# A mixture of experts on one core: experts of a chunk accumulated in one PSUM bank, with the router weight behind the GELU

## What is computed

```python
def _L0_ffn_ref(x, gate_w, gate_b, W1, b1, W2, b2):
    logits = xf @ gate_w + gate_b
    probs = jax.nn.softmax(logits, axis=-1)
    top2_vals, top2_idx = jax.lax.top_k(probs, 2)
    cw = jnp.zeros((N, Ee), dtype=xf.dtype).at[jnp.arange(N)[:, None], top2_idx].add(top2_vals)

    def step(acc, params):
        w1, bb1, w2, bb2, we = params
        h = jax.nn.gelu(xf @ w1 + bb1, approximate=False)
        y = h @ w2 + bb2
        return (acc + we[:, None] * y, None)
    out, _ = jax.lax.scan(step, jnp.zeros_like(xf), (W1, b1, W2, b2, cw.T))
...
h = h + _L0_ffn_ref(_layernorm(h, axis=-1), ...)
```

## Time and profile before

| | us |
|---|---|
| median of 3 runs | 418.08 |
| lowest of them | 417.31 |
| span of the profiled execution | 417.87 |

### The profile page before, as it was taken

The page is one execution under the profiler, slowest core; times in us unless marked ns, Lnnn a source line. Parts: engine busy times, 40 slices in busy tenths (PEclk is TensorE's granted clock), DMA queues, the critical chain, the costliest instruction groups (busy, mean ns, idle before and its releaser), DMA issues.

```text
span 417.9 us, 11928 instructions
## 1 busy us (share of the span) xinstructions
PE 359.1 (86%) x4976; PEld 247.0 (59%) x4976; DVE 226.4 (54%) x446; ACT 198.2 (47%) x382; POOL 112.6 (27%) x138
## 2 busy tenths in 40 slices
PE   4999839999997799999587947878776997999997
PEld 1447726677775534343244527878776993477774
DVE  3277797787646743333693999946663038500002
ACT  1574235444447356776747792570008645531110
POOL 9009991000000036465133026880000003000000
PEclk9999969999998699999959995999999898899999
DMA  7400012222212122121000000000000000000001
GB/s 280 192 0 2 5 38 57 60 59 59 65 54 61 55 62 59 58 64 57 20 0 0 2 0 2 3 4 5 5 5 3 3 5 0 2 0 2 0 2 71
DMA packets 20558, 14.82 MB, mean 35 GB/s; under 512 B 2329, under 2 KB 19353, under 8 KB 20377
## 3 DMA queue, kind: packets, MB, share of 16 engines
q1 hardware_dynamic: 20504, 14.07, 10.7%
HBM read 13.32 MB, written 0.74 MB: 34 GB/s over the span
## 4 chain that ended last, share of the span: by engine, by line
PE 54%; DVE 18%; POOL 11%; issue 8%; ACT 7%; DMA 1%; SPq 0%; POOLq 0%; DVEq 0%
PE PS L763 49%; POOL arena L298 7%; PE PS L827 4%; DVE arena L710 3%; DVE arena L566 2%; DVE arena L549 2%; POOL arena L321 2%; DMA arena<-xT 1%; ACT arena L356 1%; ACT arena L353 1%; POOL arena L317 1%; ACT arena L468 1%; POOL arena L316 1%; DVE arena L713 1%; ACT arena L472 1%
## 5 line engine op out<-in xcount | busy, mean ns | idle before, releaser
L763 PE MATMUL PS<-arena,K 128*128 128x360 f32 (+2 forms) x608 | 163.1, 513 | 21.5 <-DVE arena L566 6.4
L763 PE MATMUL PS<-arena 128*45 128x45 f32 (+6 forms) x3264 | 129.9, 227 | 21.3 <-ACT arena L448 9.7
L763 PEld LDWEIGHTS PS<-arena 128*45 128x45 f32 (+3 forms) x3264 | 111.7, 133 | 40.1 <-issue 23.9
L763 PEld LDWEIGHTS PS<-arena,K 128*128 128x128 f32 (+2 forms) x608 | 75.8, 183 | 82.5 <-issue 22.1
L298 POOL TENSOR_TENSOR arena<-arena 128x360 f32<-128x360 f32 x32 | 30.0, 948 | 105.9 <-DVE arena L672 105.2
L672 DVE TENSOR_TENSOR arena<-PS,arena 128x360 f32<-128x360 f32 x32 | 17.1, 533 | 33.7 <-ACT arena L402 33.7
L763 PE MATMUL PS<-K,arena 128*45 128x32 f32 (+4 forms) x768 | 26.1, 223 | 5.1 <-DVE arena L655 4.4
L763 PEld LDWEIGHTS PS<-K,arena 128*45 128x45 f32 (+2 forms) x768 | 25.3, 132 | 7.0 <-DVE arena L655 5.0
L827 PE MATMUL PS<-K,arena 128*128 128x128 f32 x128 | 21.5, 292 | 7.8 <-ACT arena L377 7.7
L756 DVE SCALAR_TENSOR_TENSOR arena<-PS,K,arena 128x360 f32<-128x360 f32 x4 | 2.4, 593 | 47.2 <-PE PS L763 47.2
L380 ACT COPY arena<-PS 128x360 f32<-128x360 f32 x32 | 14.9, 468 | 25.5 <-PE PS L827 25.4
(11 more groups left out here) (124 smaller groups left out, 422.8 us busy)
## 6 DMA issues: line engine op xcount, KB each, us to landing
WG<-wr SPq DMA_DIRECT2D x64, 64.0 KB, 1.9
arena<-wr SPq DMA_DIRECT2D x64, 64.0 KB, 1.9
arena<-xT SPq DMA_DIRECT2D x4, 368.0 KB, 6.4
K<-consts SPq DMA_DIRECT2D x1, 1171.0 KB, 12.3
K<-consts SPq DMA_DIRECT2D x1, 852.0 KB, 9.9
out<-arena SPq DMA_DIRECT2D x4, 180.0 KB, 1.9
K<-consts SPq DMA_DIRECT2D x1, 510.0 KB, 5.5
K<-consts SPq DMA_DIRECT2D x1, 352.0 KB, 12.4
```

Of the source, the lines that this page charges most:

```text
L763: return nc.tensor.matmul(o, l, r, start=start, stop=stop)
```

## The change

Chunks become the outer loop of the mixture and experts the inner; the unit (e, c) is software-pipelined with MOE_LAG = 2: in step n PE issues hid(n), y(n-2), cwb(n). Per unit:
- hid goes to one of two pairs of banks (0, 1 or 2, 3), the GELU's result to one of three pairs of slots.
- cwb becomes two bf16 matmuls with 32 rows each, one for each half, that spread the expert's weight over all 128 partitions, into banks 4 and 5. DVE multiplies the 720 hidden values by it in place. ACT's copy is gone.
- y is a pair of matmuls that accumulate on top of b2 in one bank per chunk (6 or 7), over all eight experts. DVE adds that bank to the residual once per chunk (`acc`). POOL has no part left.
- `hid` stands behind `cw2` for all experts, and `cwT` uses banks 4 to 7.

```diff
-    stage(("hid", 0), ("cwT", 0), ("cw2", 0), ("b2", 0), ("y", 0))
-    for i in range(1, E):
-        stage(("hid", i), ("y", i))
+    stage(("cwT", 0), ("cw2", 0))
+
+    moe = [(e, c) for c in range(C) for e in range(E)]
+    for n in range(len(moe) + MOE_LAG):
+        if n < len(moe):
+            order.append(("hid", *moe[n]))
+        if n >= MOE_LAG:
+            e, c = moe[n - MOE_LAG]
+            if e == 0:
+                order.append(("b2", 0, c))
+            order.append(("y", e, c))
+            if e == E - 1:
+                order.append(("acc", 0, c))
+        if n < len(moe):
+            order.append(("cwb", *moe[n]))
...
+        def hidden(i, c):
+
+            return a(c, (slot(3), slot(6), slot(8))[unit(i, c) % 3], 2 * W)
+
+        def hid_banks(i, c):
+
+            lo = 2 * (unit(i, c) % 2)
+            return PS[:, lo:lo + 2, 0:W]
+
+        def out_bank(c):
+
+            return 6 + c % 2
...
-                elif name == "y":
-                    pool.wait_ge(sem["y_mul"], n)
-                    if i:
-                        pool.wait_ge(sem["acc"], COUNT["y", i - 1, c])
-                    g.tensor_tensor(a(c, H_), a(c, H_), a(c, slot(3 + i % 2)), ALU.add).then_inc(sem["acc"], 1)
...
-                elif name == "y":
-                    act.wait_ge(sem["y_mm"], n)
-                    s.copy(a(c, slot(8)), bank(c, 1)).then_inc(sem["cwb"], 1)
...
+                elif name == "cwb":
+                    dve.wait_ge(sem["gelu"], n)
+                    dve.wait_ge(sem["cwb_mm"], n)
+                    v.tensor_tensor(halves(hidden(i, c)), halves(hidden(i, c)), PS[:, 4:6, 0:W], ALU.mult).then_inc(
+                        sem["scaled"], 1)
+                elif name == "acc":
+                    dve.wait_ge(sem["y_mm"], COUNT["y", E - 1, c])
+                    v.tensor_tensor(a(c, H_), a(c, H_), PS[:, out_bank(c), 0:W], ALU.add).then_inc(sem["acc"], 1)
...
                 elif name == "b2":
-                    pe.wait_ge(sem["c_r"], n)
-                    mm(bank(c, 0), k("b2"), a(c, slot(5))).then_inc(sem["b2_mm"], 1)
+                    if c < 2:
+                        pe.wait_ge(sem["c_r"], COUNT["cwT", 0, 2 + c])
+                    else:
+                        pe.wait_ge(sem["acc"], c - 1)
+                    mm(PS[:, out_bank(c), 0:W], k("b2"), a(c, slot(5)), stop=False)
                 elif name == "hid":
-                    if i == 0:
+                    if n == 1:
                         pe.wait_ge(sem["g_steps"], 1)
+                    if n > 2:
+                        pe.wait_ge(sem["gelu"], n - 2)
+                    for j in range(2):
+                        last = mm(hid_banks(i, c)[:, j], k("w1", i * HID, i * HID + HID, 64 * j, 64 * j + 64),
+                                  half(c, N_, j, 0, W, 64))
+                    last.then_inc(sem["hid_mm"], 1)
+                elif name == "cwb":
+                    pe.wait_ge(sem["cwT"], COUNT["cw2", 0, c])
+                    if n == 1:
+                        pe.wait_ge(sem["c_r"], C)
                     else:
-                        pe.wait_ge(sem["y_mul"], COUNT["y", i - 1, c])
-                    for j in range(2):
-                        last = mm(bank(c, j), k("w1", i * HID, i * HID + HID, 64 * j, 64 * j + 64), half(c, N_, j, 0, W, 64))
-                    last.then_inc(sem["hid_mm"], 1)
+                        pe.wait_ge(sem["scaled"], n - 1)
+                    for j in range(2):
+                        last = mm(PS[:, 4 + j, 0:W], selb[64 * j:64 * j + 32, i * 128:i * 128 + 128],
+                                  part_bf(c, 12)[64 * j:64 * j + 32])
+                    last.then_inc(sem["cwb_mm"], 1)
                 elif name == "y":
-                    if i == 0:
-                        pe.wait_ge(sem["cwT"], n)
-                        pe.wait_ge(sem["b2_add"], n)
-                    pe.wait_ge(sem["gelu"], n)
-                    for j in range(2):
-                        mm(bank(c, 0, W, 0, 64 * j, 64 * j + 64), k("w2", i * D, i * D + D), a(c, slot(6 + j)))
-                    mm(bank(c, 1), selb[:, i * 128:i * 128 + 128], part_bf(c, 12)).then_inc(sem["y_mm"], 1)
+                    pe.wait_ge(sem["scaled"], n)
+                    for j in range(2):
+                        last = mm(PS[64 * j:64 * j + 64, out_bank(c), 0:W], k("w2", i * D, i * D + D),
+                                  hidden(i, c)[:, j * W:(j + 1) * W], start=False, stop=(i == E - 1))
+                    last.then_inc(sem["y_mm"], 1)
...
-                sel[64 * j + E * part + e, e, 64 * j:64 * j + 64] = 1
+                sel[64 * j + E * part + e, e, :] = 1
```

More of the change, by code:

```diff
@@ L68 @@
 attT_mm attT wo_mm h1
-gate_mm g_sub g_exp cw cwT_mm c_hi c_r c_mid cwT b2_mm b2_add
-hid_mm gelu y_mm cwb y_mul acc
+gate_mm g_sub g_exp cw cwT_mm c_hi c_r c_mid cwT
+hid_mm gelu cwb_mm scaled y_mm acc
 delta xi xa xi_late rk_mm rk vw_mm vw aw_mm aw_aa aw_sg ab_mm ab g_hid g_sig gg_mm gg cs ep em kk0 kk_sq kk_mm kk_cl kk_ln kk_rs
@@ L78 @@
 LAG = 2
+MOE_LAG = 2
 def schedule():
@@ L215, in gate, with unit @@
             return a(0, slot(14) + C * PP * E * r, n)
+        def unit(i, c):
+            return E * c + i
+        def hidden(i, c):
[5 more added lines that the diff above has]
+            return 6 + c % 2
         def part_bf(c, i):
@@ L390, in _ @@
                     act.wait_ge(sem["cwT_mm"], n)
-                    s.copy(part_bf(c, 10), bank(c, 1)).then_inc(sem["c_hi"], 1)
+                    s.copy(part_bf(c, 10), PS[:, 4 + c, 0:W]).then_inc(sem["c_hi"], 1)
                 elif name == "cw2":
@@ L397, in _ @@
                     act.wait_ge(sem["hid_mm"], n)
-                    s.activation(halves(a(c, slot(6), 2 * W)), both(c), ACT.Gelu,
-                                 bias=k("b1", i, i + 1)).then_inc(sem["gelu"], 1)
-                elif name == "y":
-                    act.wait_ge(sem["y_mm"], n)
-                    s.copy(a(c, slot(8)), bank(c, 1)).then_inc(sem["cwb"], 1)
+                    s.activation(halves(hidden(i, c)), hid_banks(i, c), ACT.Gelu, bias=k("b1", i, i + 1)).then_inc(
+                        sem["gelu"], 1)
                 elif name == "mixes":
@@ L658, in _ @@
                     dve.wait_ge(sem["c_hi"], n)
-                    v.scalar_tensor_tensor(out=a(c, slot(5)), in0=part_bf(c, 10), scalar=vec("cw_mid"), in1=bank(c, 1),
+                    v.scalar_tensor_tensor(out=a(c, slot(5)), in0=part_bf(c, 10), scalar=vec("cw_mid"), in1=PS[:, 4 + c, 0:W],
                                            op0=ALU.mult, op1=ALU.add).then_inc(sem["c_r"], 1)
@@ L784, in _ @@
                     ready = {"lt": ("tok_y", c + 1), "l1": ("h0", c + 1), "l2": ("h1", c + 1),
-                             "l3": ("acc", COUNT["y", E - 1, c]), "gn": ("o_ev", c + 1), "l4": ("h3", c + 1)}[LNS[i]]
+                             "l3": ("acc", c + 1), "gn": ("o_ev", c + 1), "l4": ("h3", c + 1)}[LNS[i]]
                     pe.wait_ge(sem[ready[0]], ready[1])
@@ L854, in _ @@
                     pe.wait_ge(sem["cw"], n)
-                    pe.wait_ge(sem["gelu"], COUNT["hid", 0, c])
                     for p, j in pairs:
-                        last = mm(to_bank(c, 1, T, j, p, 3 * E), a(c, CW_ + 3 * p * E, 3 * E), k("identf", 64 * j, 64 * j + T))
+                        last = mm(PS[64 * j:64 * j + 3 * E, 4 + c, T * p:T * p + T], a(c, CW_ + 3 * p * E, 3 * E),
+                                  k("identf", 64 * j, 64 * j + T))
                     last.then_inc(sem["cwT_mm"], 1)
```

## The result

| | median us | ratio to before, 95% interval |
|---|---|---|
| before | 418.95 | |
| changed, first measurement | 432.37 | 1.031 (1.027 to 1.035) |
| changed, again, beside the experiments | 433.37 (before: 420.15) | 1.031 (1.027 to 1.036) |

The change makes the kernel 3.1% slower, 13 us. The forecast was 429.0 with a range of 425.0 to 434.2.

What follows compares the result with a forecast made beforehand. PE was taken to bound the mixture. To the 417.87 us span it added 10.1 (4.8 shapes, 2.6 hid round once hidden, 2.8 head's rest, fill and tail), 0.2 for the median and 0.8 for the clock: 429.0 us, range 425.0 to 434.2.

Steps and rivals of the forecast that it cites:

- The bound: Mixture before the change: PE sets the pace, busy 6.68 of 6.68 us; removing ACT and POOL work pays only at edges.
- The stream, 1.82 us a unit: Mixture's steady state on PE: hid 0.80, y 0.76, cwb 0.26, together 1.82 us a unit, 0.15 more than before.
- one hid pair alone: A pair of hid matmuls on PE with no hid before it: 0.80 us, from 2.62 - 1.82.
- 32-to-64 step free: Rival: PE's step from 32-row cwb to 64-row hid costs no shape change; -3.2 us, 425.8 us, chance 0.10.
- The spreading pair side by side: The two 32-row cwb matmuls on PE run together, at the price of the one they replace.
- The rival in sequence: The two cwb matmuls run one after the other, adding a 0.16 us pass per unit; +5.0 us, 434.0 us, chance 0.12.
- The waits: Semaphore waits in the stream, such as cwb(n) for scaled(n-1), do not bind; scaling is 0.905 us on DVE.
- The loop around it: Spreading, DVE scaling, semaphores: 1.4 us, under 1.82; the rival that it binds gave 431.3 us, chance 0.07.
- The head: Mixture's start: first hid and GELU table load come behind the cw2 casts; PE rests 2.5 us before cwb(1).
- The clock: PE's clock may halve after the head's rest, costing 1.7 us; even odds, so 0.8 us was added.
- Span and median: Whole run: the median was taken to lie 0.2 us above the profiled execution's span, so 428.0 became 428.2.
- the three b2 in the stream: Three further b2 matmuls on PE between the mixture's units, counted at 0.80 us each.

Runs made afterwards that it cites:

- e6: Kernel before with y of two chunks ahead of their two spreading matmuls, five shape changes a round instead of nine; 416.76 us, ratio 0.992.
- e7: Kernel before with each spreading matmul cut into two of 64 columns, in the shape of y; 414.41 us, ratio 0.986.
- e1: Changed kernel with spreading matmuls of 64 rows instead of 32, one shape change fewer per unit; 429.09 us, 1.015 times before.
- e3: Changed kernel with 64-row spreading, first two hid pairs under top2, units taken in pairs, five pairs of hidden slots; 420.17 us, 0.999 times before.
- e8: Kernel before with its first round of hid moved behind cw2, stream untouched; 425.38 us, ratio 1.014.
- e2: Changed kernel with the first two hid pairs ahead of cwT again, under top2; 432.89 us, 1.029 times before.

## Why the prediction came out as it did

- **The bound.** PE, not the POOL of the chain. Shown: e6 and e7 take nothing but changes of shape out of PE's stream, and the run follows.
- **The stream, 1.82 us a unit.** Measured 1.82, part by part. Adding up starts from rows made the sum right although I read one thing too small. I priced a change at 0.10, the step ahead of the next record; the other 0.10, in hid's first weights, was inside the 0.80 of "one hid pair alone", where I did not see it. e1 put the whole at 0.20 for hid, so the rival "32-to-64 step free" would have been worth 6 us and not 3.2. It did not occur: the step was charged. The Trainium skill's rule that a change of tiling mode drains the engine (TensorEngine Tiling (Array Packing), Key Properties) fits every step of both kernels: each change was charged, and e1 and e7 show the price. That the time is a drain the traces do not show.
- **The spreading pair side by side.** Its two records start together and take 0.33. The rival in sequence is out.
- **The waits.** None binds; the scaling took 0.904 us for the 0.905 of the earlier trace rows. The loop around it is 1.49 us (e3) and not 1.4, still under 1.82.
- **The head.** The rest was forecast at 2.5 and is 2.50. The table load took 1.28, with GELU 0.02 behind it, and the load followed the last cast within 0.01. By the Trainium skill (ScalarE: Activation LUTs, What ACT_TABLE_LOAD costs), which adds a drain of about 1.38 us, the GELU would have come at 147.5; it came at 146.10, so no such drain shows here either.
- **The clock, the term that was mis-sized.** I took even odds of one low stretch of 3.4 us and wrote 0.8. It fell within the rest and stayed low for 6.8 us, and cost 2.6. The rows I went by the earlier trace rows show low stretches of 3.3 and 3.4 us, as long as I had asked for, and I took that for the whole of a fall. Read in windows of 0.1 us, the first did end at 327.7, but the second went on to 358.4, 6.8 us in all: the trace of before held the length that was missed. Of the 2.1 us by which the stretch passed the forecast (13.0 against 10.1 + 0.8) 1.8 are this term; the Ln came at 215.7, not 213.8, with top2 1.0 us early.
- **Span and median.** I set the span of the profile 0.2 below the median. The executions measured after the forecast have both figures: a span of 431.9 goes with a time of 433.7, and for the kernel before 418.4 with 420.2. So 1.8 us lie around a span, and before's profiled execution was a rather long one. By ratio the change cost 3.1% where I had 2.6%; most of the 0.5% is the clock. I had counted the stages behind the Ln within 1 us; they took 2.0 more in the profile (216.2 against 214.2), which by the spread of unedited kernels (213.0 to 218.5) can't be laid to the change.
- **What is by difference.** Of the 13.0 us in the stretch 4.8 are the longer unit (32 x 0.15) and 2.6 the clock. e8 puts the lost cover at 2.7, or 3.7 with cwT equal. The other 1.9 to 2.9, the three b2 in the stream and the pipeline's fill and tail, no run isolates.

## What to carry to other kernels
On an engine that is busy throughout, price each order by the steps between unlike instructions, from start to start; nine changes of array shape in a round of 6.68 us cost 1.2 us (against 4 x 1.365 without any, an estimate from the steps), and all the copies, products and additions that hung on it cost nothing. A loop order that freed two engines which were not the bound and added changes on the busy one was a loss here, and the cheaper remedy may be to give one matmul the shape of its neighbour (e7: four lines, 1.4%). When work is moved out from under a long serial piece, count the rest that it opens on PE twice: once as time, once for the clock; and walk every engine's queue to the first operation behind it, not only the one that was last.

## What the runs showed of the hardware
- At a clock of 1.00 a change of array shape costs 0.10 us ahead of the next record for every pair of shapes seen (of 128x128, 128x64, 64x128, 32x128), and 0.10 more in the first weights of 128 fp32 columns behind it (0.05 for 64 columns); a change of type from bf16 to fp32 within a shape costs nothing (0.16 from start to start, the streaming of 360 bf16 columns, in e1 and e7).
- Spreading matmuls of 32 and of 64 rows take the same 0.33 us, and two of 64 columns beside each other take 0.32, as one of 128.
- Behind a rest of 2.50 us the clock was at 0.50 until 153.7, 6.8 us in all from within the rest (changed), and behind one of 2.09 (e2) as long. Behind one of 1.68 (e8) and one of 0.88 (e3) it stayed at 1.00. These rests had different neighbours: a rest of 0.47 and 1.1 us of work ahead of the first, a rest of 1.69 and 0.33 of work ahead of the second, 6.6 us of work ahead of the third, a rest of 1.69 and 1.5 of work ahead of the last. In the kernel before a rest of 2.56 was followed by 3.4 us at 0.50 (to 327.7) and one of 2.17 by 6.8 (to 358.4), so the rest's length alone does not give the low stretch's.
